# Wide layers take the next input's norm and modulation ahead of the output's addition, their scores use four array positions, and roots move to GpSimd's pow

## What is computed

```python
x = L0(x, c)   # h = LN(x)*g(c)+b(c); 16 heads of 16; h1 = attn + x; LN(h1) modulated again + h1
x = L1(x, c)   # 16 heads of 64, q and k normalised per head; then top-512-of-4096 routing into 8 experts
x = L2(x, c)   # 16 heads of 64, gated residual; gelu feed-forward, gated residual
x = L3(x, c)   # RMS norm, rotary, 16 heads of 16; gated feed-forward
# every normalisation: (x - mean) * rsqrt(var + 1e-5); in L1 also of q and k, over each head's 64 values
q = _ln(qkv[:, :, 0].transpose(0, 2, 1, 3), qn_g, qn_b)
attn = softmax(q @ k^T / sqrt(head width)); o = attn @ v; x = x + o @ Wout.T
```

## Time and profile before

| | us |
|---|---|
| three runs, median (lowest to highest) | 3143.8 (3141.02 to 3148.51) |
| the profiled execution | 3146.93 |
| its span | 3145.1 |
| PE busy, share of the span | 2813.3 (89%) |
| DVE, ACT, POOL busy | 1723.7, 916.6, 332.6 |
| mean granted TensorE clock | 0.949 |

### The profile page before, as it was taken

The page is one execution under the profiler, slowest core; times in us unless marked ns, Lnnn a source line. Parts: engine busy times, 40 slices in busy tenths (PEclk is TensorE's granted clock), DMA queues, the critical chain, the costliest instruction groups (busy, mean ns, idle before and its releaser), DMA issues.

```text
span 3145.1 us, 68238 instructions
## 1 busy us (share of the span) xinstructions
PE 2813.3 (89%) x27492; PEld 2032.2 (65%) x27492; DVE 1723.7 (55%) x4229; ACT 916.6 (29%) x1647; POOL 332.6 (11%) x390
## 2 busy tenths in 40 slices
PE   7999699999999933998699999998997989979999
PEld 6788556666666631665588888885443877755555
DVE  5666677777777676231444444443333888842221
ACT  2333255555555500221122222222211233311110
POOL 1111001010010101232011111110000111100000
PEclk9999799999999955999799999998998899989999
DMA  5000000000000031342300000000000000000000
GB/s 184 0 0 0 8 17 27 24 23 27 20 27 20 18 114 50 85 126 47 109 0 0 0 0 0 0 0 1 0 0 0 1 0 0 0 1 14 14 14 14
DMA packets 62313, 77.40 MB, mean 25 GB/s; under 512 B 12640, under 2 KB 52064, under 8 KB 61728
## 3 DMA queue, kind: packets, MB, share of 16 engines
q1 hardware_dynamic: 56096, 67.88, 6.5%
q0 software_dynamic: 6144, 8.52, 1.4%
HBM read 59.33 MB, written 17.06 MB: 24 GB/s over the span
## 4 chain that ended last, share of the span: by engine, by line
PE 54%; DVE 29%; issue 9%; ACT 4%; DVEq 2%; DMA 1%; POOL 0%; SPq 0%; ACTq 0%; POOLq 0%
PE psS L1079 7%; PE psW L293 6%; PE psW L286 5%; DVE work L653 5%; PE psP L463 4%; PE psP L1052 4%; PE psP L1046 4%; PE psS L1073 4%; PE psO L1046 4%; PE psO L1052 3%; DVE work L655 2%; PE psO L408 2%; PE psP L455 2%; PE psO L326 2%; PE psP L392 2%
## 5 line engine op out<-in xcount | busy, mean ns | idle before, releaser
L293 PE MATMUL psW<-r,work 128*128 128x512 f32 (+1 forms) x1280 | 557.0, 567 | 5.5 <-DVE work L690 3.7
L286 PE MATMUL psW<-work,r 128*128 128x128 f32 x3072 | 388.2, 285 | 21.7 <-DVE work L642 16.1
L286 PEld LDWEIGHTS psW<-work,r 128*128 128x128 f32 x3072 | 366.2, 198 | 42.4 <-DVE work L642 31.0
L931 ACT ACTIVATE work<-work 128x512 f32<-128x512 f32 x256 | 161.2, 630 | 628.4 <-DVE work L655 628.4
L293 PEld LDWEIGHTS psW<-r,work 128*128 128x128 f32 x1280 | 225.4, 192 | 173.3 <-issue 156.9
L979 POOL TENSOR_TENSOR work<-work 128x512 f32<-128x512 f32 x128 | 130.7, 1042 | 1274.1 <-DVE work L664 1274.1
L1079 PE MATMUL psS<-r,work 128*128 128x256 f32 x1024 | 225.3, 381 | 6.1 <-DVE work L1149 5.3
L1079 PEld LDWEIGHTS psS<-r,work 128*128 128x128 f32 x1024 | 193.2, 190 | 36.0 <-DVE work L1149 6.1
L392 PE MATMUL psP<-consts,work 128*128 128x128 f32 x1024 | 153.1, 285 | 55.7 <-ACT work L931 50.0
L655 DVE TENSOR_TENSOR work<-psS,work 128x512 f32<-128x512 f32 x256 | 177.0, 692 | 16.3
L653 DVE TENSOR_REDUCE work<-psS 128x8 f32<-128x512 f32 x256 | 174.8, 683 | 11.5 <-PE psS L372 9.7
(11 more groups left out here) (194 smaller groups left out, 4236.9 us busy)
## 6 DMA issues: line engine op xcount, KB each, us to landing
r<-in_l_fc SPq DMA_DIRECT2D x16, 1024.0 KB
work<-mod_rows SPq DMA_DIRECT2D x64, 128.0 KB, 2.9
r<-in_l_w SPq DMA_DIRECT2D x2, 3072.0 KB, 14.6
x<-in_x SPq DMA_DIRECT2D x8, 512.0 KB, 10.0
gather_table<-work SPq DMA_DIRECT2D x32, 128.0 KB, 1.8
moe_sum<-work SPq DMA_DIRECT2D x32, 128.0 KB, 1.7
x<-moe_sum SPq DMA_DIRECT2D x4, 1024.0 KB, 9.4
out<-x SPq DMA_DIRECT2D x8, 512.0 KB, 2.9
```

The lines of the kernel that those rows point to most:

```text
L286: ins = nc.tensor.matmul(ps[:, q * P:(q + 1) * P], w[:, k, lo + q * P:lo + (q + 1) * P], L.hT[:, k, :], start=(k == 0), stop=(k == KC - 1))
L293: ins = nc.tensor.matmul(ps[:, 0:width], L.hT[:, k, :], w[:, k, lo:lo + width], start=(k == 0), stop=(k == KC - 1))
L931: nc.scalar.activation(E, E, ACT.Exp, scale=scale).then_inc(L.s[f"exp{i}"].sem, 1)
```

## The change

1. In the wide layers PE transposes tile t+2 in step t, after the first half of the output product, and no longer at the head of step t+1; `pe_l2_y` is split in two for that. DVE modulates t+2 and norms t+3 at the end of step t, ahead of x1 (L1) or `dve_l2_y` (L2).
2. The wide scores alternate pairs of heads between positions (0,0), (64,64) and (0,64), (64,0); `wide_block` orders psS so that half 0 holds the even pairs and half 1 the odd ones. Their signals s0 and s1 come with the last matmuls; the product with v picks the halves to match.
3. ACT copies (and in L1 squares) the first chunk of q and k between the two exps.
4. `dve_rsqrt` is gone. GpSimd adds eps and takes the power -0.5 (`root_on_pool`: two tensor_tensor instructions); DVE asks and waits. The head roots leave the mean's 1/64 out and scale by 8 later (in `c("l1_qn")` and in rstd's copy). L0's POOL part is unrolled.

```diff
@@ -350,15 +353,20 @@
-                for j in range(HJ):
...
-                        for hp in range(2):
-                            rows = slice(64 * hp, 64 * hp + 64)
-                            ins = nc.tensor.matmul(psS[rows, (2 * j + b) * N:(2 * j + b + 1) * N],
-                                                   L.qk[rows, j, b * N:(b + 1) * N],
-                                                   L.qk[rows, HJ + j, b * N:(b + 1) * N], start=True, stop=True)
-                    if j % 4 == 3:
-                        ins.then_inc(L.s[f"s{j // 4}"].sem, 1)
+                        for odd in range(2):
+                            at = wide_block(2 * i + odd, b) * N
+                            for hp in range(2):
+                                j = 2 * i + odd
+                                rows, half = slice(64 * hp, 64 * hp + 64), 64 * (hp ^ odd)
+                                ins = nc.tensor.matmul(psS[half:half + 64, at:at + N],
+                                                       L.qk[rows, j, b * N:(b + 1) * N],
+                                                       L.qk[rows, HJ + j, b * N:(b + 1) * N], start=True, stop=True)
+                            if i == HJ // 2 - 1 and b == 1:
+                                ins.then_inc(L.s[f"s{odd}"].sem, 1)
@@ -373,6 +381,10 @@
+        def wide_block(j, b):
+            return (j % 2) * 8 + (j // 2) * 2 + b
@@ -413,15 +425,16 @@
-            for j in range(HJ):
-                if j == 4:
+            for c in range(HJ):
+                odd, j = c // 4, 2 * (c % 4) + c // 4
+                if c == 4:
...
-                        h = 2 * j + hp
+                        h, half = 2 * j + hp, 64 * (hp ^ odd)
                         ins = nc.tensor.matmul(psO[64 * hp:64 * hp + 64, b * 512 + j * N:b * 512 + (j + 1) * N],
-                                               L.v[rows, h * 64:(h + 1) * 64], L.PT[rows, j, 64 * hp:64 * hp + 64],
+                                               L.v[rows, h * 64:(h + 1) * 64], L.PT[rows, c, half:half + 64],
@@ -485,6 +498,7 @@
                     pe_wide_v(pe, L, 0, 1)
+                    pe_transpose_x(pe, L, 1)
                     if L.li == 1:
@@ -499,7 +513,7 @@
-                if ahead:
+                if ahead and not L.wide:
                     pe_transpose_x(pe, L, t + 1)
                 pe_scores(pe, L, t)
@@ -515,11 +529,14 @@
                     pe_wide_pv(pe, L, t)
                     if ahead:
                         pe_wide_v(pe, L, t + 1, 1)
+                    pe_wide_y = pe_l1_y if L.li == 1 else pe_l2_y
+                    pe_wide_y(pe, L, t, 0)
+                    if ahead >= 2:
+                        pe_transpose_x(pe, L, t + 2)
                     if L.li == 2:
-                        pe_l2_y(pe, L, t)
+                        pe_wide_y(pe, L, t, 1)
                         return
-                    pe_l1_y(pe, L, t, 0)
                     if ahead:
                         pe_l1_turn(pe, L, t + 1)
                     pe_l1_y(pe, L, t, 1)
@@ -550,27 +567,29 @@
-        def dve_rsqrt(ch, out, var):
...
-            ch.link(nc.vector.tensor_scalar(v3, var, EPS, None, ALU.add))
...
-                                            if len(shape) == 3 else q, ALU.mult))
...
+        def dve_ask_root(v, name):
+            v.sem_inc(ro["var"], 1)
+        def dve_take_root(v, name):
+            v.wait_ge(ro["root"], 2 * (ROOTS.index(name) + 1))
...
+            nc.gpsimd.tensor_tensor(out, var, const(eps), ALU.add).then_inc(done.sem, 1)
+            after(g, done, 2 * count - 1)
+            nc.gpsimd.tensor_tensor(out, out, const("minus_half"), ALU.pow).then_inc(done.sem, 1)
+        def pool_root(g, name, out, var):
+            g.wait_ge(ro["var"], ROOTS.index(name) + 1)
+            root_on_pool(g, out, var, "eps", Signal(ro["root"], 0), ROOTS.index(name) + 1)
@@ -601,28 +620,32 @@
-            dve_rsqrt(ch, rstd[:, 0:8], moments[:, 0:8, 1])
+            dve_ask_root(v, "l0 0")
+            dve_take_root(v, "l0 0")
...
-            if k == 4 or t % 8 not in (1, 3, 5):
+            if k == 4 or t % 8 not in (1, 3, 4, 5):
+                return
+            if t % 8 == 4:
+                dve_ask_root(v, f"l0 {k}")
                 return
             if t % 8 == 5:
-                dve_rsqrt(ch, rstd[:, 8 * k:8 * k + 8], moments[:, 8 * k:8 * k + 8, 1])
+                dve_take_root(v, f"l0 {k}")
...
-                var = rstd[:, :]
-            dve_rsqrt(ch, rstd[:, :], var)
+            dve_ask_root(v, name)
+            dve_take_root(v, name)
@@ -714,12 +737,11 @@
-                    nc.vector.tensor_copy(L.ss33[:, 32:33], mv[:, 0, 1:2])
-            after(v, L.s["r3"], n + 1)
-            ch.link(nc.vector.tensor_scalar(L.ss, L.ss, 1.0 / 64, None, ALU.mult))
-            dve_rsqrt(ch, L.ss33, L.ss33)
+                    nc.vector.tensor_scalar(L.ss33[:, 32:33], mv[:, 0, 1:2], 64.0, None, ALU.mult
+                                            ).then_inc(L.s["var"].sem, 1)
+            after(v, L.s["root"], (n + 1) * 2)
             if norm_too:
-                nc.vector.tensor_copy(rstd[:, bass.ds(n + 2, 1)], L.ss33[:, 32:33])
+                nc.vector.tensor_scalar(rstd[:, bass.ds(n + 2, 1)], L.ss33[:, 32:33], 8.0, None, ALU.mult)
@@ -777,12 +799,14 @@
-                    dve_rsqrt(ch, L.rstd0, moments[:, :, 1])
+                    dve_ask_root(v, "l1 all")
+                    dve_take_root(v, "l1 all")
                     for n in range(2):
                         dve_second_norm(v, ch, L, n)
-                    dve_rsqrt(ch, rstd[:, 0:2], moments[:, 0:2, 1])
+                    dve_ask_root(v, "l1 two")
+                    dve_take_root(v, "l1 two")
                 elif L.li != 0:
-                    dve_rstd(ch, rms=L.li == 3)
+                    dve_rstd(v, ch, f"l{L.li}", rms=L.li == 3)
@@ -790,6 +814,9 @@
+                if L.wide:
+                    dve_modulate(v, ch, L, 1)
+                    dve_norm(v, ch, L, 2)
@@ -800,10 +827,17 @@
+                def next_input():
+                    if ahead >= 2:
+                        dve_modulate(v, ch, L, t + 2)
+                    if ahead == 3:
+                        dve_norm(v, ch, L, t + 3)
                 ch.reset()
-                if ahead:
+                if ahead and not L.wide:
                     dve_modulate(v, ch, L, t + 1)
-                if ahead >= 2:
+                if ahead >= 2 and not L.wide:
                     dve_norm(v, ch, L, t + 2)
@@ -813,12 +847,14 @@
                         gates_before()
+                    next_input()
                     dve_l1_x1(v, ch, L, t)
                 elif L.li == 2:
...
                         x_before()
+                    next_input()
                     dve_l2_y(v, ch, L, t)
@@ -850,22 +886,23 @@
+        def act_qk(a, L, n, chunks):
+            for i in chunks:
+                after(a, L.s[f"i{i}"], n + 1)
...
                     nc.scalar.activation(L.qn[i], ps, ACT.Copy).then_inc(L.s[f"cp{i}"].sem, 1)
                     if i < 3:
@@ -931,8 +968,8 @@
                     nc.scalar.activation(E, E, ACT.Exp, scale=scale).then_inc(L.s[f"exp{i}"].sem, 1)
                     if i == 0 and behind:
                         finish(t - 1)
-                if ahead:
-                    act_qk(a, L, t + 1)
+                    if ahead:
+                        act_qk(a, L, t + 1, ACT_QK[L.li][1:] if i else ACT_QK[L.li][:1])
@@ -966,7 +1003,22 @@
+            def head_roots(n, norm_too):
+                after(g, L.s["r3"], n + 1)
+                if norm_too:
+                    after(g, L.s["var"], n + 1)
+                root_on_pool(g, L.ss33, L.ss33, "eps64", L.s["root"], n + 1)
             def first():
+                if L.li == 1:
+                    pool_root(g, "l1 all", L.rstd0, moments[:, :, 1])
+                    pool_root(g, "l1 two", rstd[:, 0:2], moments[:, 0:2, 1])
+                    head_roots(0, True)
+                if L.li == 2:
+                    pool_root(g, "l2", rstd[:, :], moments[:, :, 1])
+                if L.li == 3:
+                    pool_root(g, "l3", rstd[:, :], rstd[:, :])
@@ -978,13 +1030,23 @@
+                    if L.li == 1 and ahead:
+                        head_roots(t + 1, ahead == 3)
...
+                if L.li == 0 and t % 8 == 4 and t < NT - 8:
+                    k = t // 8 + 1
+                    pool_root(g, f"l0 {k}", rstd[:, 8 * k:8 * k + 8], moments[:, 8 * k:8 * k + 8, 1])
+            if L.li == 0:
+                first()
+                for t in range(NT):
+                    step(t, min(3, NT - 1 - t), t > 0)
+                return
@@ -1103,8 +1167,8 @@
-                    ch.link(ins)
-                    dve_rsqrt(ch, Q.stat[:, :, 2], Q.stat[:, :, 1])
+                    ins.then_inc(Q.s["f_var"].sem, 1)
+                    after(v, Q.s["f_root"], (n + 1) * 2)
@@ -1234,11 +1298,19 @@
+            def root(n, u):
```

(55 more changed lines are left out.)

26 lines of the change are left out of this document (6 added, 20 removed), and 2 rows, old and new, of the table W.

## The result

| | before | after |
|---|---|---|
| median of 4 runs (lowest to highest), us | 3146.16 (3141.02 to 3149.45) | 3169.18 (3167.49 to 3170.27) |
| span of the profiled execution, us | 3145.1 | 3165.7 |
| mean granted TensorE clock | 0.949 | 0.936 |

A forecast was written before the change was run, and what follows sets the result against it. It took PE to bound the two wide layers, L1 and L2. The terms 38 + 45 + 7 + 14 - 3 = 101 us, from the median 3143.8, gave 3042 us, range 3026 to 3060 at 0.6.

The forecast's parts named there:

- Part 1: Scores of L1 and L2 on four array positions: burst from 2.08 to 1.16 us, 0.92 us a tile, 59 us.
- Part 2: x's transposes and modulation moved in L1 and L2: with the scores, 38 us gained in L1 and 45 in L2.
- Rival A: The bank rule or another array limit keeps the scores at 2.08 us; time 3101 us; chance 0.1.
- rival D: New small waits in L1 and L2 give back 10 to 40 us; time about 3065 us; chance 0.13.
- Part 3: L1's head roots on POOL: power 1.2 us, free up to 2.5 us; beyond, each microsecond costs 31 us.
- Rival C: Slower than before: POOL's power so slow, from 5.0 us, that it eats everything; at 6 about 3180 us; chance 0.04.
- Part 4: Other roots on POOL: 14 us gained at stage heads, setup and first expert, 7 us in L0's three tiles.
- Part 5: Experts: POOL's root behind the last scatters makes PE wait 0.4 us for six or seven experts, 3 us lost.

The follow-up runs named there:

- the Newton kernel: The changed kernel with every root back on DVE by Newton's steps, new order and scores on four positions kept: 3064.12 us, ratio to before 0.9735.

## Why the prediction was wrong, step by step

- **Part 1 had the price right**: the burst is 1.16 us in both wide layers. That the gain "lies wholly on PE's path" was right only beside part 2; alone it is worth 2 us. The rule of the Trainium skill (TensorEngine Tiling (Array Packing), Gotcha 1: PSUM Pressure), that row tiles cannot access one bank at the same time, would have left it at 2.08; the pairs here share a bank, and the measurement decides against it as a price for this shape. Rival A is out.
- **Part 2 was right**: with Newton's roots the periods are 20.74 us in L1 and 18.04 in L2 (20.8 and 18.2 forecast), and the two layers give 37 and 48 us (38 and 45). None of rival D's small waits came with any weight; PE's wait for ACT inside the turned heads went from 0.42 to 0.51 us.
- **Part 3 is the step that failed**, in one term: the power on 32 or 33 columns, 1.2 us taken, 5.66 measured. The frame around it held: addition, hops and copy 0.62 us (0.65 taken), free up to 3.03 us (2.5 taken), then each microsecond 31 us. The 0.6 us that I had subtracted for later head sums was not lost: from the last sum to PE's turned heads it is 631.69 - 627.18 = 4.51 us in the kernel with Newton's roots, and it was 620.70 - 616.09 = 4.61 us, 0.15 of it a wait of PE. With 5.66 us in that frame, 31 x (5.66 - 3.03) = 82 us; the measured difference in L1 is 744.0 - 644.1 = 100. Nearly all of the other 18 is PE's clock, which fell behind two holes in three and stood nowhere in the sum: 0.7 to 0.9 us in each such tile. Rival C's own formula, with P = 5.66, gives 98 us in L1 and 27 at the heads of stages, so 3042 + 125 = 3167 us, and 3169 was measured. That this is so close is luck in part: the free length was put 0.5 us too short (16 us too much loss) and the clock was left out (18 us too little). In part 4 I had named such a drop in L0, and left it out of what a wait of PE costs in L1. The Trainium skill (Perfetto Trace Analysis, Matmul Optimizations) says that the matmul engine scales power with its utilization; 0.53 to 0.55 behind a hole of 2.4 us agrees in direction.
- Why 1.2? I wrote that the upper bound "bounds nothing in principle" and that the power is no plain arithmetic, and then took a value near the plain product's all the same. The product at 2 ns a column was the only row of POOL's arithmetic, yet it was a row for another operation. The distance was 75 times. By my own break-even of 5.0 us rival C needed 0.15 us a column, and 0.16 came. Its chance of 0.04 was a guess on a number with no bound, and the range should have held it. (The range's other end is a slip without weight: my own upper bounds add some 12 us to the sum, which is 3030 us and not 3026.)
- **Part 4**: L0's roots gave what was said: three tiles of 9.72 us stand where 11.97, 12.43 and 12.25 stood, 7.5 us (7 forecast). The rest of the 9.7 us that L0's stretch lost lies mostly in its first tile (8.84 us instead of 10.76), which other kernels with the same roots do not all have. The large roots at the heads of stages cost 6.04 us instead of 3.35, 2.7 lost each where 1.5 was to be gained. Against the Newton kernel the stretches that hold them lost 5.5 at L1 (with the first head root), 7.2 around l2ff and L3 and 1.4 at l3ff; 3.8 of the 7.2 came back in L3's first two tiles, at a higher clock (above).
- **Part 5 had the wait right and its cost partly by luck**: the experts' period went from 28.59 to 28.95 us, some 2.5 us in all for the 3 forecast. But the power on 4 columns alone takes 1.04 us, where 0.4 was taken; the root ends 1.37 us behind the last scatter (1382.53 to 1383.90 in one expert), where I had put 0.9 for issue, addition, power and hops. I had put the wait at 0.4 us although my own times gave less than 0.1 (1294.9 + 2.0 against 1296.83), and that reserve took it up.
- **L3** has a tile of 10.70 us where 10.60 stood, about 3 us. It goes with the head roots of L1's loop on POOL, in every kernel that has them there: whole, on 16 or 24 columns, in quarters, and with the roots alone. It is 10.60 in each kernel without. The tenth stands ahead of DVE's modulation, and PE's q and k wait 0.15 us instead of 0.04. Why L3 should feel a root of L1 was not found.

## What to carry over

An operation that no row of the trace prices has no middle value. If the sum turns on it, work out its break-even, give the side beyond it real weight, and measure the operation by itself before anything is built on it. Ask of each step not how long it takes but who waits for it and since when: the same power, more work in four pieces, cost nothing once it ran under other work, and a matmul burst cut by half gave nothing until the chain that it had covered was moved. Two parts of a change can be worth 2 and 26 us alone and 83 together, so test the pair before either is dropped.

## What the hardware showed that I had not expected

- POOL's power of two tensors takes 0.70, 1.04, 1.73, 2.13, 2.90, 4.17, 5.43 and 5.66 us on 2, 4, 8, 9, 16, 24, 32 and 33 columns of 128 partitions, about 0.16 us a column; its addition on 33 columns takes 0.24. The Trainium skill (GPSIMD Engine Reference, 3.1 Elementwise) prices an addition at 4497 ns for 2048 columns, 2.2 ns a column; the products here (1042 ns on 512, 2.0 ns a column) agree. The power is some 75 times that. Fifteen Newton instructions on DVE did the same 33 columns in 3.3 us (627.21 to 630.54 in the kernel with all roots by Newton).
- An idle time of PE of 2.4 us in each tile brought the granted clock behind it down to 0.53 to 0.55 in two tiles of three, one of 0.95 us left it at 1.00.
- 64 score matmuls of 64 x 64 whose pairs share a PSUM bank (other partitions of it) from different rows of the array run in 1.16 us, no slower than the products with v, whose banks follow the rows.
